# Gate rows by one transfer per expert, the second attention's outputs of every second group taken earlier, and the convolution's spectrum computed beside the gathers

## Chip, cores and metric

The kernel runs on one core of one Trainium2 chip, in single precision. The metric is the device time of one execution in microseconds (us), the median of several runs. Lower is better.

## What is computed

A two-layer decoder on x (4 sequences of 512 tokens, 256 features), with a layer norm after each residual sum:

```python
x = _layernorm(x + _L0_attn_ref(x, ...))      # attention among a token's 16 heads
x = _layernorm(x + _L0_xattn_ref(ctx, x, ...)) # cross attention to 64 context rows
x = _layernorm(x + _L0_ffn_ref(x, ...))       # 8 experts, two per token
x = _layernorm(x + _L1_attn_ref(x, ...))      # causal, 16 heads, top 64 scores kept, heads mixed before and after
x = _layernorm(x + _L1_xattn_ref(x, ctx, ...)) # modulation, S4D convolution, an MLP of 1024
x = _layernorm(x + _L1_ffn_ref(x, ...))       # 64 small experts, eight per token, plus 2 shared experts
```

Three places matter here. The last feed-forward part computes, for every token, all 64 experts of width 64 (silu(x W1 + b1) W2) and weighs each with the token's gate, which is zero for all but eight. The second attention mixes the 16 heads' scores with a 16x16 matrix, keeps the 64 largest of each row, and mixes the heads again after the softmax. The S4D part convolves the sequence with a kernel K of 512 positions by 256 features; that is done by a discrete Fourier transform as a matrix product, for which the spectrum of K (1024 rows: real and imaginary parts) is needed.

## The kernel before

The program is a row of stages, each a block in which all engines run their own instruction stream, with a barrier at the end. Semaphores order the engines within a block. SyncE (SP) issues nearly all DMAs, in the order of its program; a wait on it holds up everything behind it.

**Combining stage of the first feed-forward part** (`l0_combine`, line 2514). GpSimd issues 32 gathers of 128 rows of 1 KB (line 2528). TensorE meanwhile sums the convolution kernel K from small factors (512 matmuls with 16 columns, line 2538); VectorE copies each of 8 groups to `kl` (line 2547). Then VectorE weighs the gathered rows (lines 2553 and 2557). SyncE writes `kl` to DRAM (line 2563).

**Second attention** (`l1_attention`, from line 1502). Each batch has four tiles of 128 queries. A group is one tile; `ORDER = (0, 3, 1, 2)` gives the tiles at positions 0 to 3, so the narrowest tile (keys 24 to 144) comes first. A group has 8 steps (`STEPS1`), each with a pair of row blocks of 128 rows (8 queries by 16 heads). In step k TensorE mixes the scores of pair k+2 (`mix`), does side work (`l1_units`: projections, values and scores of tiles to come), transposes the pair k-2 with the second mixing (`post`, line 1745), and then takes finished groups' products: `heads` (attention weights times values, lines 1763 and 1767) and `output` (lines 1778 to 1780: eight products with the output weights, the bias, the residual). ScalarE does the matching copies in the same order; the copy of an output is line 1909, and `mixed_out` (line 1861) stands behind it in the next step. VectorE searches the 64 largest (lines 2049 to 2074), GpSimd masks (lines 2003, 2011). Two functions set when the products of a group come: `l1_heads(k)` and `l1_outs(k)` (lines 1483 and 1496). A group at position 0 has its heads in steps 2 to 5 and its output in step 6 of the next group; a group at another position has its heads in steps 1 to 7 of the next group and its output in step 0 of the one after that. The last group's products come at the end.

**Spectrum** (`s4d_spectrum`, line 2088). A stage of its own after the second attention's norm: SyncE loads `kl` back (512 KB) and the transform's matrix `dft` (2 MB), TensorE multiplies them in 8 groups of 4 products (line 2115; each shows as two matmul records), ScalarE copies each group to `kf` (line 2106). `modulation_attention` (line 2120) follows.

**Last stage** (`l1_tail`, line 2594). First the MLP of the modulated branch (hidden products line 2780, output line 2794), with the router between. ScalarE's first copy to `xT` (line 2883) waits for all twelve loads counted on `small_in`. Then a loop over 4 batches of 40 items: 8 of the shared experts and 32 pairs of small experts. Of one item TensorE computes the hidden values (line 2807: 128 hidden rows, two experts of 64, by 512 tokens), ScalarE applies the activation (line 2912), VectorE multiplies by the gates for a pair (line 3043), and TensorE adds the output product (line 2826) two items later. After the last item of a batch comes the bias product (line 2832). The gates stand in DRAM as one row of 512 values for each expert; for each pair SyncE copies two of them, each onto 64 partitions, into one of four buffers (line 2717). It may do so once the pair four earlier has been multiplied (semaphore `ready`). SyncE's same program stores the gates of batches 1 to 3 (line 2699) and writes the results of finished batches (line 2703).

Of the kernel before, what the change touches and what calls it, by code (L numbers as in the profile page):

```python
# [7 lines left out]
F32 = mybir.dt.float32  # L8
# [6 lines left out]
P = 128  # L15
B, S, D = 4, 512, 256
NT = S // P
# [1465 lines left out]
def l1_heads(k):  # L1483

    n = k // STEPS1 - 1
    s = k % STEPS1
    if n < 0 or n >= GROUPS1:
        return []
    if n == GROUPS1 - 1:
        return [(n, j) for j in range(8)] if s == 1 else []  # L1490
    if n % NT == 0:
        return [(n, 2 * (s - 2) + a) for a in range(2)] if 2 <= s < 6 else []
    return [] if s == 0 else [(n, s - 1)] if s < STEPS1 - 1 else [(n, s - 1), (n, s)]


def l1_outs(k):

    n, s = k // STEPS1 - 1, k % STEPS1
    if n >= 0 and n % NT == 0 and s == 6:
        return [n]  # L1500
    if n >= 1 and s == 0 and (n - 1) % NT != 0 and n - 1 < GROUPS1 - 1:
        return [n - 1]
    return []
# [584 lines left out]
def s4d_spectrum(nc, G, kf):  # L2088

    with ExitStack() as ctx:  # L2090
        sb, ps, sem = buffers(nc, ctx, "ss")
        kl = sb("kl", [P, NT, D])
        dft = sb("dft", [P, NT, 2 * FR])
        pf = [ps(f"pf{i}", [P, 512]) for i in range(2)]
        loaded, spectrum, stored = sem("loaded"), sem("spectrum"), sem("stored")
        with nc.Block() as block:
            @block.sync
            def _(sp):
                sp.dma_start(kl[:], G.s4d_positions.rearrange("p (j d) -> p j d", j=NT)).then_inc(loaded, 16)
                sp.dma_start(dft[:], G.dram["c_dft"].rearrange("(k p) f -> p k f", p=P)).then_inc(loaded, 16)  # L2100

            @block.scalar
            def _(act):
                for n in range(2 * FT):
                    act.wait_ge(spectrum, n + 1)
                    act.copy(kf[:, n, :], pf[n % 2][:, 0:D]).then_inc(stored, 1)

            @block.tensor
            def _(pe):
                pe.wait_ge(loaded, 32)  # L2110
                for m in range(2 * FT):
                    if m >= 2:
                        pe.wait_ge(stored, m - 1)
                    for k in range(NT):
                        ins = pe.matmul(pf[m % 2][:, 0:D], dft[:, k, m * P:(m + 1) * P], kl[:, k, :],
                                        start=(k == 0), stop=(k == NT - 1))
                    ins.then_inc(spectrum, 1)


def modulation_attention(nc, G, cT):  # L2120

    with ExitStack() as ctx:
# [26 lines left out]
        dve_steps, mixed, cstored = sem("dve_steps"), sem("mixed"), sem("cstored")  # L2149
# [13 lines left out]

# [336 lines left out]
def l1_modulated(nc, G):  # L2500
    d = G.dram
    with ExitStack() as ctx:
        kf = ctx.enter_context(nc.sbuf_tensor("l1_kf", [P, 2 * FT, D], F32))
        s4d_spectrum(nc, G, kf)
        cT = ctx.enter_context(nc.sbuf_tensor("l1_cT", [P, KD, B * S], F32))
        modulation_attention(nc, G, cT)
# [7 lines left out]
def l0_combine(nc, G, R, K):  # L2514

    with ExitStack() as ctx:
        sb, ps, sem = buffers(nc, ctx, "sp")
        kl = sb("kl", [P, NT, D])
        pk = [ps(f"pk{i}", [LO, 32, HI]) for i in range(2)]
        summed, copied, stored, weighed = sem("summed"), sem("copied"), sem("stored"), sem("weighed")  # L2520
        N = D // 32
        y = R.w1[:].rearrange("p e k f -> p (e k f)")[:, 0:TOP0 * TT * D].rearrange("p (n t d) -> p n t d", n=TOP0, t=TT)
        with nc.Block() as block:
# [67 lines left out]
def l1_tail(nc, G, store):  # L2591


    with ExitStack() as ctx:
# [33 lines left out]
        mlp_in, expert_in, w2_in, small_in = sem("mlp_in"), sem("expert_in"), [sem(f"w2_in{i}") for i in range(2)], sem("small_in")  # L2628
# [38 lines left out]
        with nc.Block() as block:  # L2667
            @block.sync
            def _(sp):
                sp.dma_start(wm1[:], d["L1_xattn_W1"].rearrange("(k p) n -> p k n", p=P)).then_inc(mlp_in, 16)  # L2670
                sp.dma_start(wm2[:], d["L1_xattn_W2"].rearrange("(k p) n -> p k n", p=P)).then_inc(mlp_in, 16)
                with nc.allow_non_contiguous_dma(reason="biases and gains onto partitions"):
                    for i, v in enumerate(("L1_xattn_g_ffn", "L1_xattn_b_ffn")):
                        sp.dma_start(gf[:, i, :], d[v].rearrange("(k p) -> p k", p=P)).then_inc(small_in, 16)
                    sp.dma_start(bm1[:], d["L1_xattn_b1"].rearrange("(k p) -> p k", p=P)).then_inc(small_in, 16)
# [30 lines left out]
                for r in range(B * PAIRS):  # L2706
# [19 lines left out]
            def _(pool):  # L2726
                pool.memset(cw[E1:, :], 1.0).then_inc(ones, 1)
                pool.wait_ge(ones, 1)
                pool.wait_ge(small_in, 16 * 12)
# [6 lines left out]
            def _(pe):  # L2736
# [108 lines left out]
                pe.wait_ge(small_in, 16 * 12)  # L2845
# [24 lines left out]
            def _(act):  # L2870
# [45 lines left out]
                act.wait_ge(small_in, 16 * 12)  # L2916
# [18 lines left out]
                turned("n2", 2)  # L2935
                for x in range(B * ITEMS):
# [15 lines left out]
            def _(dve):  # L2952
# [99 lines left out]
                dve.wait_ge(small_in, 16 * 12)  # L3052
# [29 lines left out]
def build(nc, dram, out):  # L3082
    with ExitStack() as ctx:
        G = Shared(nc, ctx, dram)
        G.s4d_positions = nc.dram_tensor("s4d_positions", (P, NT * D), F32).ap()
# [40 lines left out]
```

## Time and profile before

| | |
|---|---|
| median of 3 runs | 4064.18 us (4058.31 to 4065.22) |
| the profiled execution's own time | 4035.73 us |
| its span | 4033.9 us |
| mean granted TensorE clock | 0.811 of full speed |
| TensorE matmuls busy | 2853.6 us (71%) |
| VectorE busy | 2492.0 us (62%) |
| ScalarE busy | 1079.2 us (27%) |
| GpSimd busy | 975.2 us (24%) |
| DMA | 234.80 MB, mean 58 GB/s |

The stages that the change touches, by the timeline:

| stage | from, us | to, us |
|---|---|---|
| combining | 1025.8 | 1075.5 |
| second attention | 1097 | 2670 |
| spectrum | 2688.0 | 2714.7 |
| modulation's attention | 2714.7 | about 2881 |
| last stage, MLP | 3138.6 | 3291 |
| last stage, items of 4 batches | 3291 | 4025.2 |

Busy times are sums over stages with different limits, so they don't say what an edit is worth. The chain of waits, the timeline around a boundary and the table of stretches do. Full speed of TensorE's clock is 2.4 GHz; the other level is half of it.

### The profile page before, as it was taken

To read this page: it belongs to the slowest core of one execution; us is meant where nothing else is said; L and a number is where in the kernel's file an instruction comes from. 1 tells how busy PE (TensorE), PEld (TensorE's weight loads), DVE (VectorE), ACT (ScalarE), POOL (GpSimd) and SP (SyncE) were. 2 spreads that over 40 slices of the span, in tenths; PEclk is the share of its full clock that TensorE was granted. 3 is DMA by queue.
4 is the path that set the end of the run, shared out by engine and by line. 5 is a ranking of instruction groups with operands and counts; after the bars stand their busy time and mean duration, and the time that the engine had idled before them with its cause. 6 is when DMAs were issued, how large, how long until landed. Compare 5 with 4: busy or idle time off the path is not lost. (4 is left out here: it accounts for less than half of the span.)

```text
span 4033.9 us, 40612 instructions
## 1 busy us (share of the span) xinstructions
PE 2853.6 (71%) x11696; PEld 1813.1 (45%) x11696; DVE 2492.0 (62%) x7770; ACT 1079.2 (27%) x2754; POOL 975.2 (24%) x1217
## 2 busy tenths in 40 slices
PE   4755982999586777577767766453279798878686
PEld 2323552676443445355445544341124465545453
DVE  4995654454329998998999899938744251111111
ACT  1013550343033333333333433211100231111111
POOL 2650003000314544454445445410031100000000
PEclk6657995999667788786878786775589899999998
DMA  2000003555232111212212211000010311111111
GB/s 83 0 0 14 6 1 136 160 164 169 83 101 69 55 64 57 84 41 77 71 53 64 69 58 45 19 31 1 9 53 0 89 58 53 45 54 45 54 49 46
DMA packets 177338, 234.80 MB, mean 58 GB/s; under 512 B 32089, under 2 KB 135197, under 8 KB 177118
## 3 DMA queue, kind: packets, MB, share of 16 engines
q1 hardware_dynamic: 174046, 223.81, 17.0%
q0 software_dynamic: 3072, 8.39, 0.7%
q8 instruction: 97, 1.59, 0.2%
q14 instruction: 123, 1.01, 0.1%
HBM read 170.56 MB, written 61.60 MB: 58 GB/s over the span
## 5 line engine op out<-in xcount | busy, mean ns | idle before, releaser
L2062 DVE MATCH_REPLACE8 a_rest<-a_best,a_rest 128x416 f32<-128x416 f32 (+54 forms) x1308 | 606.1, 472 | 0.0
L2070 DVE MAX8 a_best<-a_rest 128x8 f32<-128x416 f32 (+54 forms) x1308 | 567.4, 476 | 0.0
L3043 DVE TENSOR_TENSOR tl_hT<-tl_act_out,tl_gate 128x512 f32<-128x512 f32 x128 | 88.6, 692 | 570.2 <-DMA tl_gate<-l_gates 450.6
L1745 PE MATMUL a_pat<-a_kp,a_probs 128*128 128x128 f32 x1344 | 281.7, 380 | 210.9 <-POOL a_kp L1964 205.6
L1745 PEld LDWEIGHTS a_pat<-a_kp,a_probs 128*128 128x128 f32 x1344 | 248.9, 277 | 292.1 <-POOL a_kp L1964 267.9
L2003 POOL TENSOR_SCALAR a_probs<-a_mixed,a_best 128x120 f32<-128x120 f32 (+12 forms) x208 | 285.9, 1375 | 329.3 <-DVE a_best L2074 308.5
L2826 PE MATMUL tl_py<-tl_w,tl_hT 128*128 128x256 f32 x1024 | 258.5, 397 | 139.0 <-DVE tl_hT L3043 139.0
L1726 PE MATMUL a_psc<-a_kT,branch 64*128 64x264 f32 (+3 forms) x640 | 226.0, 609 | 182.5 <-ACT a_stage L1828 181.8
L2826 PEld LDWEIGHTS tl_py<-tl_w,tl_hT 128*128 128x128 f32 x1024 | 192.2, 194 | 251.0 <-DVE tl_hT L3043 209.9
L1726 PEld LDWEIGHTS a_psc<-a_kT,branch 64*128 64x128 f32 x640 | 118.7, 261 | 273.1 <-ACT a_stage L1828 247.2
L2807 PE MATMUL tl_ph<-xT,tl_w 128*128 128x512 f32 x512 | 240.8, 593 | 0.0
L1736 PE MATMUL a_pmix<-a_rows,a_kpre 128*128 128x264 f32 (+41 forms) x528 | 183.1, 475 | 79.1 <-ACT a_mixed L1861 74.5
L1964 POOL TENSOR_SCALAR a_kp<-a_kpost,a_rden 128x128 f32<-128x128 f32 x256 | 152.6, 608 | 318.1 <-DVE a_rden L2033 318.0
L2912 ACT ACTIVATE tl_act_out<-tl_ph,tl_b 128x512 f32<-128x512 f32 x128 | 88.0, 687 | 493.3 <-PE tl_ph L2807 490.5
L1880 ACT ACTIVATE a_probs<-a_probs,a_negmax 128x72 f32<-128x72 f32 (+28 forms) x232 | 126.2, 545 | 332.5 <-POOL a_probs L2011 329.7
L2011 POOL TENSOR_TENSOR a_probs<-a_mixed,a_probs 128x72 f32<-128x72 f32 (+28 forms) x232 | 185.0, 818 | 9.3
L2049 DVE MAX8 a_best<-a_mixed 128x8 f32<-128x24 f32 (+28 forms) x232 | 95.4, 454 | 116.6 <-ACT a_negmax L1868 58.4
L1414 DVE COPY xT<-f_pT 128x512 f32<-128x512 f32 x78 | 50.3, 686 | 174.5 <-PE f_pT L1346 174.5
L1736 PEld LDWEIGHTS a_pmix<-a_rows,a_kpre 128*128 128x128 f32 x528 | 98.8, 222 | 118.9 <-issue 109.1
L1828 ACT COPY a_stage<-a_psc 128x264 f32<-128x264 f32 (+3 forms) x320 | 112.1, 381 | 127.0 <-PE a_psc L1726 121.7
L1336 PE MATMUL f_ph<-f0o_w,f_xsT 128*128 x312 | 142.8, 601 | 0.6 <-issue 0.6
L1356 PE MATMUL f_py<-f_w,xT 128*128 128x256 f32 x624 | 141.1, 379 | 0.5 <-DVE xT L1414 0.5
(421 smaller groups left out, 5309.5 us busy)
## 6 DMA issues: line engine op xcount, KB each, us to landing
f_w<-in_L_ffn_W SPq DMA_DIRECT2D x39, 1024.0 KB, 5.7
tl_gate<-l_gates SPq DMA_DIRECT2D x128, 256.0 KB
l_scores<-a_stage SPq DMA_DIRECT2D x32, 528.0 KB, 2.7
l_scores<-a_stage SPq DMA_DIRECT2D x32, 400.0 KB, 2.4
l_scores<-a_stage SPq DMA_DIRECT2D x32, 272.0 KB, 2.1
f0o_w<-in_L_ffn_W SPq DMA_DIRECT2D x8, 1024.0 KB, 12.5
sorted_x<-z_blank SPq DMA_DIRECT2D x1, 4992.0 KB, 17.0
f_xs<-sorted_x SPq DMA_DIRECT2D x39, 128.0 KB, 5.3
```

What stands on the lines that cost most here:

```text
L1336: ins = pe.matmul(ph[half][:], xsT[:, j % 2, k, :], w, start=(k == 0), stop=(k == KD - 1))
L1356: ins = pe.matmul(py[j % 2][:], hT[j % 2][:, f, :], w2[:, j % 2, f, :], start=(f == 0), stop=(f == FT - 1))
L1726: full(pe.matmul(out[:, 0:hi - lo], qT[r, j, i * P:(i + 1) * P], kT[r, j, lo:hi], start=True, stop=True))
L1736: ins = pe.matmul(pmix[:, at, 0:hi - lo], kpre[:], rows[:, g % 4, lo:hi], start=True, stop=True)
L1745: ins = pe.matmul(pat[:, at + c, :], probs[:, g % 4, c * P:(c + 1) * P], kp[:, g % 4, :], start=True, stop=True)
L1964: pool.tensor_scalar(kp[:, g % 4, :], kpost[:], rden[:, g % 4:g % 4 + 1], None, ALU.mult).then_inc(kp_ready, 1)
L2003: ins = pool.tensor_scalar(p, x, best[:, a, LAST, 7:8], HIDE, ALU.is_lt, ALU.mult)
L2011: pool.tensor_tensor(p, x, p, ALU.add).then_inc(masked, 1)
L2062: last[a] = signal(dve.match_replace(rest[:, a, 0:wd], best[:, a, q - 1, :], rows_of[a] if q == 1 else rest[:, a, 0:wd], GONE))
L2070: last[a] = signal(dve.max(best[:, a, q, :], rest[:, a, 0:wd]))
L2807: ins = pe.matmul(ph[m % 2][:], lhsT, G.xT[:, k, b * S:(b + 1) * S], start=(k == 0), stop=(k == KD - 1))
L2826: ins = pe.matmul(py[t][:, 0:D], src[:, t * P:(t + 1) * P], w, start=(n == 0), stop=False)
```

## The change

Five edits in one file:
1. The gates of a pair are copied by two transfers, one per expert, each from one row of 512 values onto 64 partitions; VectorE waits for 32 instead of 16 on the buffer's semaphore.
2. In `l1_heads` and `l1_outs` the test `n % NT == 0` becomes `n % 2 == 0`: groups at position 2 follow the scheme of position 0.
3. The spectrum's products and copies move into `l0_combine`; `kl` isn't written to DRAM any more, the spectrum (1 MB) is.
4. The spectrum's stage goes, and `modulation_attention` loads `kf` behind its own loads, with a wait at the end of SyncE's program.
5. In `l1_tail` the three small loads that ScalarE's first copy needs are issued first and counted on a semaphore of their own.

```diff
@@ l1_heads, l1_outs
-    if n % NT == 0:
+    if n % 2 == 0:
         return [(n, 2 * (s - 2) + a) for a in range(2)] if 2 <= s < 6 else []
...
-    if n >= 0 and n % NT == 0 and s == 6:
+    if n >= 0 and n % 2 == 0 and s == 6:
         return [n]
-    if n >= 1 and s == 0 and (n - 1) % NT != 0 and n - 1 < GROUPS1 - 1:
+    if n >= 1 and s == 0 and (n - 1) % 2 != 0 and n - 1 < GROUPS1 - 1:
         return [n - 1]
@@ s4d_spectrum
-def s4d_spectrum(nc, G, kf):
...
@@ modulation_attention, behind the masks' loads
+                sp.dma_start(kf[:].rearrange("p n d -> p (n d)"), G.s4d_spectrum).then_inc(kf_in, 16)
+                sp.wait_ge(kf_in, 16)
@@ l0_combine
+        room = R.w1[:].rearrange("p e k f -> p (e k f)")
+        Y, T = TOP0 * TT * D, NT * 2 * FR
+        y = room[:, 0:Y].rearrange("p (n t d) -> p n t d", n=TOP0, t=TT)
+        dft = room[:, Y:Y + T].rearrange("p (k f) -> p k f", k=NT)
+        kf = room[:, Y + T:Y + T + 2 * FT * D].rearrange("p (n d) -> p n d", d=D)
...
+                pe.wait_ge(dft_in, 16)
+                pe.wait_ge(copied, N)
+                for m in range(2 * FT):
+                    if m >= 2:
+                        pe.wait_ge(kept, m - 1)
+                    for k in range(NT):
+                        ins = pe.matmul(pf[m % 2][:, 0:D], dft[:, k, m * P:(m + 1) * P], kl[:, k, :],
+                                        start=(k == 0), stop=(k == NT - 1))
+                    ins.then_inc(spectrum, 1)
+            @block.scalar
+            def _(act):
+                for m in range(2 * FT):
+                    act.wait_ge(spectrum, m + 1)
+                    act.copy(kf[:, m, :], pf[m % 2][:, 0:D]).then_inc(kept, 1)
...
-                sp.wait_ge(copied, N)
-                sp.dma_start(G.s4d_positions, kl[:].rearrange("p j d -> p (j d)")).then_inc(stored, 16)
+                sp.dma_start(dft, G.dram["c_dft"].rearrange("(k p) f -> p k f", p=P)).then_inc(dft_in, 16)
+                sp.wait_ge(kept, 2 * FT)
+                sp.dma_start(G.s4d_spectrum, kf.rearrange("p n d -> p (n d)")).then_inc(stored, 16)
                 sp.wait_ge(stored, 16)
@@ l1_tail, SyncE
+                    for i, v in enumerate(("L1_xattn_g_ffn", "L1_xattn_b_ffn")):
+                        sp.dma_start(gf[:, i, :], d[v].rearrange("(k p) -> p k", p=P)).then_inc(gain_in, 16)
+                    sp.dma_start(bm1[:], d["L1_xattn_b1"].rearrange("(k p) -> p k", p=P)).then_inc(gain_in, 16)
                 sp.dma_start(wm1[:], d["L1_xattn_W1"].rearrange("(k p) n -> p k n", p=P)).then_inc(mlp_in, 16)
                 sp.dma_start(wm2[:], d["L1_xattn_W2"].rearrange("(k p) n -> p k n", p=P)).then_inc(mlp_in, 16)
-                        sp.dma_start(gf[:, i, :], d[v].rearrange("(k p) -> p k", p=P)).then_inc(small_in, 16)
-                    sp.dma_start(bm1[:], d["L1_xattn_b1"].rearrange("(k p) -> p k", p=P)).then_inc(small_in, 16)
...
-                    sp.dma_start(gate[:, r % 4, :],
-                                 G.l1_gates[b, 2 * n:2 * n + 2, :].unsqueeze(1).to_broadcast([2, F1, S])
-                                 ).then_inc(gate_in[r % 4], 16)
+                    for e in range(2):
+                        sp.dma_start(gate[F1 * e:F1 * e + F1, r % 4, :], G.l1_gates[b, 2 * n + e].partition_broadcast(F1)
+                                     ).then_inc(gate_in[r % 4], 16)
@@ l1_tail, ScalarE (and TensorE, GpSimd, VectorE: 16 * 12 becomes 16 * 9)
-                act.wait_ge(small_in, 16 * 12)
+                act.wait_ge(gain_in, 48)
                 turned("nf", 0)
...
                 turned("n2", 2)
+                act.wait_ge(small_in, 16 * 9)
                 for x in range(B * ITEMS):
@@ l1_tail, VectorE
-                    dve.wait_ge(gate_in[r % 4], 16 * (r // 4 + 1))
+                    dve.wait_ge(gate_in[r % 4], 32 * (r // 4 + 1))
```

## Rows read from the trace of the kernel before

**Rows 1.** The chain that ended last, last stage: start us, us, what.

```profile
3345.19 1.73 PE tl_py L2826 x8
...
3472.05 1.99 PE tl_py L2826 x8
...
3654.50 1.99 PE tl_py L2826 x8
...
3659.94 1.73 PE tl_py L2826 x8
3663.38 1.73 PE tl_py L2826 x8
...
3836.49 1.99 PE tl_py L2826 x8
...
4018.00 3.78 PE tl_py L2826 x8
4021.78 3.43 PE tl_py L2832 x8
```

**Rows 2.** Stretches, last stage: length, busy PE, PEld, DVE, ACT, POOL, clock, DMA share, GB/s.

```profile
3462.00:3472.00 10.00, 6.78 (x23) 3.80 (x21) 1.38 (x2) 1.38 (x2) 0.00 (x0) 1.00 0.13 49
...
3510.00:3654.00 144.00, 109.04 (x353) 66.15 (x352) 18.93 (x28) 20.62 (x30) 0.00 (x0) 0.99 0.14 53
```

**Rows 3.** ScalarE at a batch boundary (start us, us, instruction), then a line of waits.

```profile
1524.64 0.61 ACT L1880 ACTIVATE a_probs<-a_probs,a_negmax 128x376 f32<-128x376 f32 x1 [3.52 <-POOL a_probs L2011]
...
1539.91 0.62 ACT L1880 ACTIVATE a_probs<-a_probs,a_negmax 128x392 f32<-128x392 f32 x1 [2.60 <-POOL a_probs L2011]
...
1549.90 0.37 ACT L1909 COPY x<-a_pO 128x256 f32<-128x256 f32 x1 [4.63 <-PE a_pO L1780]
...
ACT x L1909 <- PE a_pO L1780: 72.8, 16, 5.3
```

**Rows 4.** Timeline of SyncE, first issue of the spectrum's stage and of the next.

```profile
2687.97 0.32 SPq L2099 DMA_DIRECT2D ss_kl<-s4d_positions  x1
...
2714.72 0.38 SPq L2155 DMA_DIRECT2D ma_wq<-in_L_xattn_Wq  x1
```

**Rows 5.** Timeline, first 20 us of the last stage.

```profile
3139.53 0.57 SPq L2674 DMA_DIRECT2D tl_gf<-in_L_xattn_g_ffn  x1
...
3141.93 3.43 SPq L2676 DMA_DIRECT2D tl_b<-in_L_ffn_b  x1
...
3147.63 0.21 ACT L2875 ACTIVATE tl_std<-tl_rstd 128x12 f32<-128x12 f32 x1 [6.73 <-DVE tl_rstd L2963]
...
3157.76 1.45 ACT L2883 ACTIVATE xT<-tl_pT,tl_gf 128x512 f32<-128x512 f32 x2 [9.91 <-DMA tl_b<-in_L_ffn_sb]
```

**Rows 6.** DMA issues: destination and source, queue, count, KB of each, us to landing.

```profile
tl_wm<-in_L_xattn_W SPq DMA_DIRECT2D x2, 1024.0 KB, 6.5
...
s4d_positions<-sp_kl SPq DMA_DIRECT2D x1, 512.0 KB, 2.8
...
xa_bo<-in_L_xattn_bo SPq DMA_DIRECT2D x1, 128.0 KB, 2.9
```

**Rows 7.** Line 2717 (shortest, median and longest issue in ns), then one issue in the timeline.

```profile
L2717 SPq DMA_DIRECT2D tl_gate<-l_gates x128: 482/5222/6296, 3296.6 to 3997.5; - x128
...
3318.47 0.48 SPq L2717 DMA_DIRECT2D tl_gate<-l_gates  x1
```

**Rows 8.** Stretches (columns as in rows 2), combining stage and the spectrum's products.

```profile
1040.00:1054.00 14.00, 12.68 (x238) 12.57 (x236) 4.81 (x18) 0.00 (x0) 10.41 (x12) 0.50 0.36 105
...
2697.00:2701.00 4.00, 4.00 (x10) 3.19 (x11) 0.00 (x0) 0.28 (x1) 0.00 (x0) 0.50 0.00 0
2701.00:2714.00 13.00, 12.76 (x56) 10.76 (x54) 0.00 (x0) 2.53 (x8) 0.00 (x0) 0.94 0.00 0
```

**Rows 9.** Timeline, end of the combining stage.

```profile
1053.91 0.32 SPq L2563 DMA_DIRECT2D s4d_positions<-sp_kl  x1
...
1069.10 6.42 DVE L2557 SCALAR_TENSOR_TENSOR branch<-f0o_w,f0o_gates,branch 128x256 f32<-128x256 f32 x16
```

More of the change, by code:

```diff
@@ L2085, with modulation_attention @@
 FT = FR // P
-def s4d_spectrum(nc, G, kf):
[L2090 to L2120, printed above, removed]
+def modulation_attention(nc, G, cT, kf):
     with ExitStack() as ctx:
@@ L2148, in modulation_attention @@
             sem("scored"), sem("shifted"), sem("exped"), sem("meaned"), sem("turned"), sem("stored"))
-        dve_steps, mixed, cstored = sem("dve_steps"), sem("mixed"), sem("cstored")
+        dve_steps, mixed, cstored, kf_in = sem("dve_steps"), sem("mixed"), sem("cstored"), sem("kf_in")
         d = G.dram
@@ L2503, in l1_modulated @@
         kf = ctx.enter_context(nc.sbuf_tensor("l1_kf", [P, 2 * FT, D], F32))
-        s4d_spectrum(nc, G, kf)
         cT = ctx.enter_context(nc.sbuf_tensor("l1_cT", [P, KD, B * S], F32))
-        modulation_attention(nc, G, cT)
+        modulation_attention(nc, G, cT, kf)
         norm_stage(nc, G, "ni", add=False, turn=False, dst=G.branch)
@@ L2519, in l0_combine @@
         pk = [ps(f"pk{i}", [LO, 32, HI]) for i in range(2)]
+        pf = [ps(f"pf{i}", [P, 512]) for i in range(2)]
         summed, copied, stored, weighed = sem("summed"), sem("copied"), sem("stored"), sem("weighed")
+        dft_in, spectrum, kept = sem("dft_in"), sem("spectrum"), sem("kept")
         N = D // 32
-        y = R.w1[:].rearrange("p e k f -> p (e k f)")[:, 0:TOP0 * TT * D].rearrange("p (n t d) -> p n t d", n=TOP0, t=TT)
+        room = R.w1[:].rearrange("p e k f -> p (e k f)")
[3 more added lines that the diff above has]
+        kf = room[:, Y + T:Y + T + 2 * FT * D].rearrange("p (n d) -> p n d", d=D)
         with nc.Block() as block:
@@ L2627, in l1_tail @@
         pT = [ps(f"pT{i}", [P, S]) for i in range(2)]
-        mlp_in, expert_in, w2_in, small_in = sem("mlp_in"), sem("expert_in"), [sem(f"w2_in{i}") for i in range(2)], sem("small_in")
+        mlp_in, expert_in, w2_in = sem("mlp_in"), sem("expert_in"), [sem(f"w2_in{i}") for i in range(2)]
+        gain_in, small_in = sem("gain_in"), sem("small_in")
         moments, rooted, h_ready, x_ready = sem("moments"), sem("rooted"), sem("h_ready"), sem("x_ready")
@@ L2669, in _ @@
             def _(sp):
+                with nc.allow_non_contiguous_dma(reason="biases and gains onto partitions"):
+                    for i, v in enumerate(("L1_xattn_g_ffn", "L1_xattn_b_ffn")):
+                        sp.dma_start(gf[:, i, :], d[v].rearrange("(k p) -> p k", p=P)).then_inc(gain_in, 16)
+                    sp.dma_start(bm1[:], d["L1_xattn_b1"].rearrange("(k p) -> p k", p=P)).then_inc(gain_in, 16)
                 sp.dma_start(wm1[:], d["L1_xattn_W1"].rearrange("(k p) n -> p k n", p=P)).then_inc(mlp_in, 16)
                 sp.dma_start(wm2[:], d["L1_xattn_W2"].rearrange("(k p) n -> p k n", p=P)).then_inc(mlp_in, 16)
-                with nc.allow_non_contiguous_dma(reason="biases and gains onto partitions"):
-                    for i, v in enumerate(("L1_xattn_g_ffn", "L1_xattn_b_ffn")):
-                        sp.dma_start(gf[:, i, :], d[v].rearrange("(k p) -> p k", p=P)).then_inc(small_in, 16)
-                    sp.dma_start(bm1[:], d["L1_xattn_b1"].rearrange("(k p) -> p k", p=P)).then_inc(small_in, 16)
+                with nc.allow_non_contiguous_dma(reason="biases onto partitions"):
                     sp.dma_start(b1[:], d["L1_ffn_b1"].rearrange("(n a) h -> (a h) n", a=2)).then_inc(small_in, 16)
@@ L2728, in _ @@
                 pool.wait_ge(ones, 1)
-                pool.wait_ge(small_in, 16 * 12)
+                pool.wait_ge(small_in, 16 * 9)
                 for b in range(B):
@@ L2844, in _ @@
                 turn("n2", 0)
-                pe.wait_ge(small_in, 16 * 12)
+                pe.wait_ge(small_in, 16 * 9)
                 scores(0)
@@ L3051, in _ @@
                     normal_h(b)
-                dve.wait_ge(small_in, 16 * 12)
+                dve.wait_ge(small_in, 16 * 9)
                 dve.wait_ge(biased, 1)
@@ L3084, in build @@
         G = Shared(nc, ctx, dram)
-        G.s4d_positions = nc.dram_tensor("s4d_positions", (P, NT * D), F32).ap()
+        G.s4d_spectrum = nc.dram_tensor("s4d_spectrum", (P, 2 * FT * D), F32).ap()
         G.sorted_x = nc.dram_tensor("sorted_x", (SLOTS * P, D), F32).ap()
```

## The prediction

> **What bounds the kernel now.** I read the chain that ended last, then the stretches it names. Its largest link is the transfer of the gates in the last stage, and the chain's rows give a ruler for it: the output product of one item (line 2826) starts every 3.44 us where only TensorE sets the pace (3659.94 to 3663.38) [rows 1]. The last products of the four batches start at 3472.05, 3654.50, 3836.49 and 4018.00: 182.45, 181.99 and 181.51 us for 40 items each, or 4.55 us an item. So TensorE waits there. The table of stretches says for what [rows 2]: between 3510 and 3654 it is busy 109 of 144 us at a granted clock of 0.99, while the DMA engines are busy 0.14 and move 53 GB/s. One gate transfer is 256 KB, so at that rate it takes 4.9 us, and 5.3 at the 49 that the shorter stretches show; VectorE's product waits for it. A share of 0.14 is about two of sixteen engines (0.125): the source's slowest dimension is 2 (two experts), its next 64. Two engines are full and fourteen idle.
>
> In the second attention the timeline shows a different bound: VectorE's search, except where one batch ends and the next begins with the narrowest tile. There TensorE computes the output of the third group, ScalarE waits for it, and the narrow tile's rows wait behind ScalarE [rows 3]. The spectrum's stage [rows 4] has nothing beside it. At the last stage's start ScalarE waits for twelve small loads of which it needs three [rows 5].
>
> **Gates.** 128 transfers of 2x64 rows become 256 of 64 rows of 2 KB. If the slowest dimension sets the number of engines, as the two busy ones say, 64 rows can lie on all sixteen, four on each. I cost the pace at TensorE's 3.44 us, if the pair of transfers lands in less. Bounds for the pair: a broadcast of 128 KB onto 128 partitions landed 2.9 us after its issue [rows 6]; two in flight at once take that, two strictly in turn 5.8. They are issued up to four items ahead (13.8 us), so latency is covered and only the rate counts; the pair of 1024 KB loads landed in 6.5 us [rows 6], or 1.6 for each 256 KB, latency and all. I take the pace as TensorE's, nearer 2.9, and keep the other end for a rival. SyncE: an issue that finds room takes 0.48 us, though the median of the 128 is 5.22 [rows 7]; I read the 5.22 as standing in a full queue, since the same instruction was short where it had waited for a buffer. Two are 0.96 of 3.44 us. The three stores of gate weights and the four stores of results stand in the same queue and get short with it; VectorE's wait for 32 instead of 16 queues nothing else.
>
> A batch then takes 39 x 3.44 plus the 5.44 us between 3654.50 and 3659.94, where the bias product lies: 139.6 us. Savings: 182.45 - 139.6 = 42.9, then 42.4 and 41.9. In the first batch I count 26 steps of one item from 3345.19 to 3472.05: 126.86 - 26 x 3.44 = 37.4, less 1 for the transposes of weights between them: 36.4. At the very end TensorE runs at the half clock, since it had waited: the last two groups took 3.78 and 3.43 us, the first of them 1.99 at the end of the other batches [rows 1]. Half of 7.2, 3.6, is gained. Sum **167.2**.
>
> Against it stands a rule. The Trainium skill, "DMA: Bandwidth & Descriptors", rules for kernel authors, says that two transfers to disjoint partition halves are not worth it, as both spray over the same engines and serialize. The same list says that a small slowest dimension confines a transfer to that many engines. The share of 0.14 [rows 2] speaks for the second; the first would leave this term at nothing, and it is a rival below.
>
> **Attention.** In groups at position 2 of four, the heads move from steps 1 to 7 to two each in steps 2 to 5 of the following group, and the output from the next group's step 0 to step 6. Nothing is added: 16 products with the weights, the bias and the residual, one ScalarE copy. Before, ScalarE sat idle 4.63 us for it at 1549.90 and then copied for 0.37; all sixteen outputs took 72.8 us of such waits, none over 5.3 [rows 3]. Four of them are moved from exposed places, three at boundaries and one in the drain, where the last posts queue behind it on TensorE: 4 x 5.0 = 20.0.
> The new place is covered by VectorE's search, whose steps are 15 us long there (1524.64 to 1539.91). At those two points ScalarE waits 3.52 and 2.60 us for GpSimd's mask [rows 3]; the output's 5.0 at the end of step 6 uses these up, but step 7 loses two heads and a copy. What could be late next is the narrow tile's first mixed rows. I give back 1 us over all: **19**. Bounds: 0 (the wait merely moves) and 21; a loss if TensorE there is at the half clock, 10 us for an output instead of 5, of which 4 could show at each of four places.
>
> **Spectrum.** Removed: the stage from SyncE's first issue at 2687.97 to the next stage's first at 2714.72 [rows 4], **26.75** us, nothing lying beside it. The next stage's first products wait for their own loads as before. Added there: a load of 1024 KB behind the masks' loads on SyncE, with a wait at the end of its program; its landing, 6.5 us by the load of that size [rows 6], lies in the stage that begins at 2714.72 and is 166 us long by the table of stages. Added in the combining stage: the load of 2 MB, the 32 products (two matmul records each), 8 copies and a store of 1 MB. The load has the 28 us from the stage's start to 1053.9; the gathers are paced by GpSimd's issue, and it can push the early ones only. The products start when VectorE's last copy is done (SyncE's issue at 1053.91 marks it) and there, as in the removed stage, they begin at the half clock, 0.50 [rows 8]. In the removed stage they took 4.00 + 12.76 us of TensorE, 0.50 in the first part and 0.94 in the second [rows 8]; with the last copy 17.2. So 1071.1, then issue and landing of the store: 2.8 us by the 512 KB stored here before, 6.5 by the load of 1024 [rows 6]; I take 4.6, halfway: 1076. VectorE is done at 1069.10 + 6.42 = 1075.5 [rows 9]. Cost **1**. If the clock stayed low, the work of 4.00 x 0.50 + 12.76 x 0.94 = 14 us at full clock would take 28, ending at 1087: 11. At best it is 0; a gain is excluded, since VectorE's part is untouched.
>
> **Small loads.** ScalarE's wait goes from 3157.76 to where the second root is done, 3147.63 + 0.21 [rows 5]: 9.9. The weights of the first layer are issued 2.4 us later (the moved issues filled 3139.53 to 3141.93), so the second leaves at 3141.4 and lands, by the same pair's 6.5 us [rows 6], at 3147.9; TensorE needs them when ScalarE's 1.45 us are over, at 3149.3. Descriptors of 4 bytes ahead of them may cost a microsecond. Gain **9**, between 5 and 9.9. The rest of the stage follows TensorE, so it shifts whole. GpSimd and VectorE still wait for the nine others, needed 30 us later.
>
> **Sum.** 167.2 + 19 + 26.75 - 1 + 9 = 221 of the profiled run's 4035.7 (span 4033.9 and 1.8 around it): 3814.7. The three runs have a median of 4064.2, 28.5 above the profiled one; I carry that over: 3843. Were the 28.5 all in slower gate transfers, 3815.
>
> **Rivals.**
> 1. *Gates half freed*: many engines read one 2 KB row of DRAM, and a pair takes 4.4 us. For: 2.9 us for 128 KB is more than bytes explain. Against: it contains the fixed latency. Against 5.3 now and 3.44 forecast that loses half of 167: 3927.
> 2. *Nothing gained at the gates*: the two halves go through the same engines one after the other, so the pair takes 5.3 us as before; only 54 of gain are left: 4010. Against: fourteen idle engines. It is the first rule's case.
> 3. *The output only moves its wait*: VectorE starved in step 7, or the boundary late. Gain 0 to -16 in the attention: 3862 to 3878. For: slack of 2.6 and 3.5 us only. Against: the step loses two heads.
> 4. *Slower*: the 5.22 us of an issue are SyncE's own work for a broadcast, not a full queue. Two are 10.4 us an item, 128 items 1336 us instead of some 722: 614 - 54 more, 4624. It decides from 3.0 us an issue, where two would take 5.6 us, today's pace (722 / 128), and the 0.4 of an item that the 54 give. For: the median. Against: the issues of 0.48.
> 5. *The spectrum does not fit*: half clock, 11 us, and the last gather delayed by 4: 3857.
>
> **How the numbers follow.** Forecast 0.76, rivals 1: 0.07, 2: 0.05, 3: 0.06, 4: 0.02, 5: 0.04. The range takes the forecast with its bounds and rivals 3 and 5: down to 3808 (the 28.5 and a few us of the bounds), up to 3878. Rivals 1, 2 and 4 with 0.14 are outside. A measurement tells 0.2%, 8 us. Only rival 4 is slower; 0.01 for mishaps that cancel. Faster 0.97.
>
> **What would show it.** In the profile after: gate issues of 0.5 us, outputs every 3.44 us throughout and 139.6 us between the last products of two batches; VectorE waiting for ScalarE's activations, not for gates; DMA share above 0.14 with twice the transfers; no output of TensorE in the narrow tile's step 0; combining stage ended 0 to 2 us later; the modulation's stage begun 0.3 us after the norm; the first hidden product 10 us earlier. Outputs at 5.34 would refute the reading of the engines, issues of 5 us that of the queue.

## The result, and the profile after

The changed kernel takes **3853.62 us** (median of 4 runs, 3849.98 to 3853.76), the kernel before 4064.70 beside it (4058.31 to 4069.04): a ratio of 0.948, 95% interval 0.9468 to 0.9492. The forecast was 3843, its range 3808 to 3878. The profiled execution took 3853.54 us.

| profile of | before | after |
|---|---|---|
| the execution's time | 4035.73 us | 3853.54 us |
| its span | 4033.9 us | 3851.7 us |
| mean granted TensorE clock | 0.811 | 0.800 |
| TensorE matmuls busy | 2853.6 us (71%) | 2838.4 us (74%) |
| VectorE busy | 2492.0 us | 2491.4 us |
| DMA | 234.80 MB, 58 GB/s | 235.88 MB, 61 GB/s |

Between these two profiles lie 182 us, between the medians 211. That difference is the main finding, and comes last here.

**Last stage.** The chain of waits of the kernel after, as [rows 1] (L2819 is the output product, L2825 the bias product):

```profile
3421.15 1.73 PE tl_py L2819 x8
3424.59 1.73 PE tl_py L2819 x8
3426.32 1.73 PE tl_py L2825 x8
3429.76 1.73 PE tl_py L2819 x8
...
3565.78 1.73 PE tl_py L2825 x8
...
3705.24 1.73 PE tl_py L2825 x8
...
3841.28 1.74 PE tl_py L2825 x8
```

Outputs come every 3.44 us, batches every 139.46, 139.46 and 136.04 us. The stretch of the second batch (columns as in [rows 2]), then the gates' issues (as [rows 7]) with their time to landing, then the waits of VectorE's product:

```profile
3430.00:3564.00 134.00, 134.00 (x468) 88.66 (x468) 25.19 (x45) 29.40 (x42) 0.00 (x0) 1.00 0.20 67
```
```profile
L2711 SPq DMA_DIRECT2D tl_gate<-l_gates x256: 444/592/1489, 3285.0 to 3824.3; - x128
...
DMA to landing us min/median/max: 2.7/2.9/4.0
```
```profile
DVE tl_hT L3037 <- ACT tl_act_out L2905: 385.8, 126, 14.1
```

TensorE is busy all of the 134 us. An issue lasts 0.59 us instead of 5.22, with twice as many of them, and a gate row lands in 2.9 us. VectorE waits for ScalarE's activations alone.

**Attention.** ScalarE at the same boundary as [rows 3]:

```profile
1564.43 0.37 ACT L1909 COPY x<-a_pO 128x256 f32<-128x256 f32 x1 [5.54 <-PE a_pO L1780]
...
1578.01 0.62 ACT L1880 ACTIVATE a_probs<-a_probs,a_negmax 128x392 f32<-128x392 f32 x1 [2.57 <-POOL a_probs L2011]
...
1583.28 0.34 ACT L1861 ACTIVATE a_mixed<-a_pmix 128x56 f32<-128x56 f32 x2
```

The narrow tile's row of 56 keys in the kernel before:

```profile
1550.17 0.34 ACT L1861 ACTIVATE a_mixed<-a_pmix 128x56 f32<-128x56 f32 x2
```

The output is now copied at 1564.43, ahead of step 7. From the activation of 392 keys to the narrow tile's mixed row of 56 keys it takes 5.27 us; before, the output stood between them and it took 10.26 (1539.91 [rows 3] to 1550.17).

**Combining stage.** The stretches of line 2513, the 512 small products (length, busy PE, PEld, clock, DMA share, GB/s), and the stage's end:

```profile
1026.00:1036.00 10.00, 4.50 (x59) 3.62 (x57) 0.50 0.81 303
1036.00:1066.00 30.00, 3.43 (x22) 2.29 (x22) 0.50 0.36 105
1066.00:1076.00 10.00, 6.87 (x121) 6.66 (x122) 0.50 0.01 2
1076.00:1090.00 14.00, 14.00 (x266) 14.00 (x265) 0.50 0.01 2
```
```profile
1091.58 16.57 PE L2522 MATMUL sp_pf<-sp_kl,f0o_w 128*128 128x256 f32 x64 [1.35 <-DVE sp_kl L2537]
...
1095.67 6.41 DVE L2547 SCALAR_TENSOR_TENSOR branch<-f0o_w,f0o_gates,branch 128x256 f32<-128x256 f32 x16
...
1108.59 0.32 SPq L2554 DMA_DIRECT2D s4d_spectrum<-f0o_w  x1
...
1113.35 1.23 DVE L143 TENSOR_TENSOR x<-x,branch 128x1024 f32<-128x1024 f32 x1 [11.27 <-PEq L82]
```

Only 22 products run in the 30 us from 1036, and the last 266 run in 14 us. The products take 66.0 us (1024.0 to 1090.0); in the profile of before they took 26.7 (1025.8 to 1052.5). The spectrum's products follow, and the next stage's addition begins at 1113.35, where it had begun at 1076.31.

**Modulation's stage and the MLP's start.** The first issues, the load of the spectrum and the first products; then the last stage's start, as [rows 5]:

```profile
2710.95 0.38 SPq L2123 DMA_DIRECT2D ma_wq<-in_L_xattn_Wq  x1
...
2712.73 2.43 SPq L2129 DMA_DIRECT2D ma_tmask<-in_mask_BxS_bf  x4
2715.20 0.57 SPq L2131 DMA_DIRECT2D l_kf<-s4d_spectrum  x1
...
2721.57 4.88 PE L2142 MATMUL ma_pp<-xT,ma_wq 128*128 128x512 f32 x7 [11.50 <-DMA ma_tmask<-in_mask_BxS_bf]
```
```profile
3137.11 0.38 SPq L2664 DMA_DIRECT2D tl_gf<-in_L_xattn_g_ffn  x1
...
3146.16 0.21 ACT L2868 ACTIVATE tl_std<-tl_rstd 128x12 f32<-128x12 f32 x1 [6.74 <-DVE tl_rstd L2957]
3146.28 1.43 ACT L2876 ACTIVATE xT<-tl_pT,tl_gf 128x512 f32<-128x512 f32 x2
...
3147.86 2.90 PE L2773 MATMUL tl_ph<-xT,tl_wm 128*128 128x512 f32 x3 [4.78 <-ACT xT L2876]
```

In the kernel before, the last stage's first issue was not the one that [rows 5] begin with but that of the MLP's weights, 0.94 us earlier:

```profile
3138.59 0.38 SPq L2670 DMA_DIRECT2D tl_wm<-in_L_xattn_W  x1
```

The MLP's first product comes 10.75 us behind the stage's first issue; it was 20.76 (3159.35, 3138.59). The first products of the modulation's attention come 10.6 us behind theirs; in the trace of before they began at 2722.03, 7.3 us behind [rows 4].

### The profile page after: what moved, and what is told of

Its sections match the earlier page's. It is cut to its first block and busy times, and to the rows that moved or that the text cites. A ratio compares the mean times of both kernels' runs of the same rounds, so it can differ in the third digit from the quotient of the medians.

```text
span 3851.7 us, 40732 instructions
## 1 busy us (share of the span) xinstructions
PE 2838.4 (74%) x11696; PEld 1831.2 (48%) x11696; DVE 2491.4 (65%) x7770; ACT 1078.0 (28%) x2754; POOL 976.2 (25%) x1217
## 2 busy tenths in 40 slices
DMA packets 181179, 235.88 MB, mean 61 GB/s; under 512 B 35929, under 2 KB 139037, under 8 KB 180702
## 5 line engine op out<-in xcount | busy, mean ns | idle before, releaser
L1745 PE MATMUL a_pat<-a_kp,a_probs 128*128 128x128 f32 x1344 | 295.7, 395 | 206.1 <-POOL a_kp L1964 201.1
L1745 PEld LDWEIGHTS a_pat<-a_kp,a_probs 128*128 128x128 f32 x1344 | 262.4, 291 | 287.5 <-POOL a_kp L1964 263.4
L2819 PE MATMUL tl_py<-tl_w,tl_hT 128*128 128x256 f32 x1024 | 241.6, 379 | 0.0
L2819 PEld LDWEIGHTS tl_py<-tl_w,tl_hT 128*128 128x128 f32 x1024 | 194.6, 190 | 80.2 <-issue 60.0
## 6 DMA issues: line engine op xcount, KB each, us to landing
f_w<-in_L_ffn_W SPq DMA_DIRECT2D x39, 1024.0 KB, 5.6
f0o_w<-in_L_ffn_W SPq DMA_DIRECT2D x8, 1024.0 KB, 12.6
```

Source lines behind the costliest of these rows:

```text
L1745: ins = pe.matmul(pat[:, at + c, :], probs[:, g % 4, c * P:(c + 1) * P], kp[:, g % 4, :], start=True, stop=True)
L2819: ins = pe.matmul(py[t][:, 0:D], src[:, t * P:(t + 1) * P], w, start=(n == 0), stop=False)
```

## The experiments

They ran in three series, each with its own runs of the kernel before. The median of those was 4062.61 us (7 runs) beside experiments 1 to 4, 4035.13 (13 runs) beside 5 to 8, and 4034.48 (6 runs) beside 9 to 12. The changed kernel takes 3853.62 us beside the first of these medians and 3812.72 beside the last (experiment 9). The expectations of 5 to 8 add to 3853.6, but these four ran in the second series, so their differences are taken here from 3812.72. Stage lengths come from the timelines; "combining" is from the first small product to the addition of the next stage.

**1. The kernel before again** (no edit).

> The kernel before, unchanged, to see its combining stage a second time. In the profile of before TensorE's 512 small products took 27 us and the stage 50.5 us to the norm's first addition; in the changed kernel the same products took 65 us, idle up to 2.6 us before each with nothing shown that they wait for, until the last gather had landed, and the stage took 89. Theory A (the gathers hold up TensorE's stream of instructions, and the profile of before was the exception): the small products take 60 to 66 us here too, the stage 77 to 80, and the time is near 4064, not 4036. Theory B (the new load of 2 MB causes the hold-up): products 27 us, stage 50.5, time near 4036 or a difference elsewhere.

4064.21 us, a single run. The same line (L2538 here) in its trace:

```profile
1036.00:1066.00 30.00, 3.27 (x21) 2.12 (x19) 0.50 0.34 101
1066.00:1076.00 10.00, 7.80 (x139) 7.49 (x139) 0.50 0.01 2
```

Where the profile of before has 313 products in those 30 us, this one of the same kernel has 21. Its combining stage takes 78.9 us instead of 50.5. The 28.4 us are the size of the 28.5 that the forecast had carried over without a cause (the other stages differ by up to 5.6 us and sum to 0.3), and they aren't the change's doing. Small products that stand idle like this are called the hold-up below.

**2. Spectrum undone**: the stage of its own, the store of `kl` and its reload are back, the rest stays changed.

```diff
+        s4d_spectrum(nc, G, kf)
-                sp.dma_start(kf[:].rearrange("p n d -> p (n d)"), G.s4d_spectrum).then_inc(kf_in, 16)
```

> The changed kernel with the spectrum back in its own stage; gates, attention and small loads stay changed. Theory A: the small products are held up as in the changed kernel; the stage loses only the spectrum behind them, 89 to some 78 us, and the spectrum's stage costs 26.75 again: 3853.6 + 26.8 - 11 = 3869. Theory B: the stage is back at 50.5 us: 3853.6 + 26.8 - 38.8 = 3841.6.

3862.76 us, ratio 0.951 (0.9494 to 0.9526). Combining takes 78.9 us; from the attention's last output to the modulation's first issue 44.8 us pass instead of 17.5, and from there to the MLP 433.5 instead of 436.9. So here the moved spectrum costs 89.35 - 78.9 = 10.4 us, gains 27.3, and the load of `kf` costs 3.4. Theory A holds; its 3869 is 6 too high for that load and for an attention of 1556.1 us against 1559.4.

**3. The transform's matrix loaded late**: the 2 MB only when the last small product is done.

```diff
+                sp.wait_ge(summed, N)
                 sp.dma_start(dft, G.dram["c_dft"].rearrange("(k p) f -> p k f", p=P)).then_inc(dft_in, 16)
```

> The changed kernel, with the load of the transform's matrix issued only when TensorE's small products are done. Theory A: they are held up by the gathers all the same until some 45 us after the stage's start; then the load (9 us) comes on top of the path: 3853.6 to 3862. Theory B: products in 27 us, load 9, spectrum 17, store 5: a stage of about 60 instead of 89, 3825.

3856.81 us, 0.9497 (0.9481 to 0.9513). The small products still take 66.1 us, with 22 of them in the 30 us from 1036: the 2 MB load doesn't hold TensorE up. Loaded late it only delays the spectrum, and combining takes 96.2 us. That is theory A.

**4. The gathers issued late**: after the last small product.

```diff
+                pool.wait_ge(summed, N)
                         pool.indirect_dma_start(y[:, n, t, :], None, G.sorted_y,
```

> The changed kernel, with GpSimd's gathers begun only when TensorE's small products are done; the load of 2 MB stays at the start. Theory A: products in 27 us although the load runs beside them; the gathers then take 27 to 69 us, the spectrum's products are held up by them in turn, and the stage ends after 76 to 91 us: 3840 to 3856. Theory B: the products are held up for the 10 us of the load and no longer: 37 us, then gathers to 79, stage 87 or more: 3851 or more.

**3841.00 us**, 0.9459 (0.9444 to 0.9475). Line 2514 here, with no gather beside it and the 2 MB load running:

```profile
1024.00:1036.00 12.00, 12.00 (x229) 12.00 (x228) 0.50 0.45 175
1036.00:1066.00 30.00, 13.53 (x254) 13.42 (x252) 0.69 0.19 54
```

All 512 are done in 26.5 us (1022.8 to 1049.3) and combining takes 77.15 us, though the gathers begin only then. So the gathers are what holds TensorE up, and where they do, this order beats both kernels: 12.6 us below the 3853.62 of the changed one.

TensorE isn't the only engine that stands still. Three of ScalarE's eight copies of the spectrum, which now run beside the gathers (in brackets the idle time before each; "remote" is the profile's word where it finds no engine or transfer of the kernel that released it):

```profile
1065.29 0.37 ACT L2531 COPY f0o_w<-sp_pf 128x256 f32<-128x256 f32 x1 [5.06 <-remote]
1074.44 0.37 ACT L2531 COPY f0o_w<-sp_pf 128x256 f32<-128x256 f32 x1 [8.78 <-remote]
1093.34 0.37 ACT L2531 COPY f0o_w<-sp_pf 128x256 f32<-128x256 f32 x1 [18.52 <-remote]
```

In experiment 11, with the same order and no hold-up, these copies come every 1.73 us. Here TensorE runs the first six groups of the spectrum in 12.4 us beside the gathers, and then it is TensorE that waits for ScalarE, 7.15 us before the last group. The copy at 1093.34 is of the seventh group, whose products had ended at 1067.71; the last gather is issued at 1088.62. The stage is hardly longer for it, 77.15 us here and 77.1 there: the store of the spectrum, issued at 1095.22, now ends it, at nearly the time when VectorE, which waits for the gathers until 1091.35, is done (1098.8).

**5. Gates undone**: one transfer of 2x64 rows for a pair again, and a wait for 16.

```diff
-                    for e in range(2):
-                        sp.dma_start(gate[F1 * e:F1 * e + F1, r % 4, :], G.l1_gates[b, 2 * n + e].partition_broadcast(F1)
+                    sp.dma_start(gate[:, r % 4, :],
+                                 G.l1_gates[b, 2 * n:2 * n + 2, :].unsqueeze(1).to_broadcast([2, F1, S])
```

> The changed kernel with one transfer of two rows per pair again, all else as changed. Theory (two engines of sixteen carry it): the 167 us come back, 3853.6 + 167 = 4021, with VectorE waiting for gates and a DMA share of 0.14 in the items. Rival (part of the gain belongs to the shorter queue for stores and results, or to the clock): less than 150 comes back.

3982.19 us, 0.9869 (0.9852 to 0.9885). The gates' issues and VectorE's wait, as before the change:

```profile
L2710 SPq DMA_DIRECT2D tl_gate<-l_gates x128: 482/5222/6372, 3244.1 to 3946.0; - x128
```
```profile
DVE tl_hT L3037 <- DMA tl_gate<-l_gates: 450.9, 97, 5.9
```

From the MLP's start to the last bias product 864.5 us, against 695.7 in experiment 7 beside it: the gates are worth 168.8 (169.5 in the medians). Less than 150 was the rival, and it falls.

**6. Attention undone**: the two functions with `% NT` again.

```diff
-    if n % 2 == 0:
+    if n % NT == 0:
```

> The changed kernel with position 2's heads and outputs where they were. Theory (four exposed outputs of 5 us): 3853.6 + 19 = 3872.6; the interval may tell 16 from 22. Rival (the output only moved its wait): 3854 to 3858. The second attention took 1578 us in the kernel before run again and 1555 to 1559 in four runs with the change, so I lean to 19 or a little more.

3834.44 us, 0.9503 (0.9487 to 0.9519). From the attention's first load of weights to its last output 1575.3 us, against 1557.0 to 1557.4 in experiments 5, 7, 8 and 9: 18 us (21.7 in the medians).

**7. ScalarE waits for all small loads again.**

```diff
+                act.wait_ge(small_in, 16 * 9)
```

> The changed kernel, where ScalarE waits for all twelve small loads again before its first copy in the last stage; their order stays changed. Theory: the wait alone is worth the 9 to 10 us: 3863. Rival (the order of the loads did it, or the weights of the MLP come later anyway): 3854 to 3857.

3826.17 us, 0.9485 (0.9469 to 0.9501). From the modulation's first issue to the MLP 448.3 us, against 436.6 to 436.8 in experiments 5, 6 and 8: in this order of loads the wait is worth 11.6 (13.5 in the medians). That is more than the change gained here, because the new order makes it longer: the first hidden product comes 22.51 us behind the stage's first issue, against 20.76 in the kernel before and 10.74 without the wait.

**8. Two transfers of 2x32 rows** for a pair, each from one row as in the change, but with a slowest dimension of 2.

```diff
-                        ... G.l1_gates[b, 2 * n + e].partition_broadcast(F1)
+                        ... G.l1_gates[b, 2 * n + e].unsqueeze(0).unsqueeze(0).to_broadcast([2, F1 // 2, S])
```

> The changed kernel with two transfers for a pair as changed, but each source written as 2 x 32 repetitions of the row instead of 64, so that its slowest dimension is 2. Theory (the slowest dimension sets the number of engines): back to two engines, the pace of an item 5.3 us or more, about 4021 us, DMA share 0.14. Rival (having two transfers in flight is what helps): as changed, 3854, DMA share the same as in the changed kernel. If the two repeated dimensions are folded into one of 64 before they reach the queue, this run tells nothing and shows 3854 too.

4005.57 us, 0.9939 (0.9922 to 0.9955). Issues, wait and a stretch (columns as in [rows 2]):

```profile
L2711 SPq DMA_DIRECT2D tl_gate<-l_gates x256: 482/2551/3787, 3243.5 to 3975.0; - x128
```
```profile
DVE tl_hT L3037 <- DMA tl_gate<-l_gates: 477.4, 99, 6.2
```
```profile
3462.00:3580.00 118.00, 95.97 (x315) 59.03 (x313) 15.91 (x23) 18.35 (x27) 0.00 (x0) 0.99 0.14 50
```

As many transfers as in the change, as many bytes, and a DMA share of 0.14 again: it isn't the number of transfers that frees the gates but their shape. This one is 24.5 us slower in the stage than the single transfer (889.0 against 864.5).

**9. The changed kernel again** (no edit).

> The changed kernel once more, on the chip of the next three kernels. Theory: there are two kinds of chip or run. Where the kernel before has its median near 4035, the 512 small products beside the gathers take 27 us, the combining stage 50.6 us and this kernel about 3816 (ratio 0.9455); where it has its median near 4063, they take 65 us, the stage 89 us and this kernel 3853 (ratio 0.948). Rival: the 28.5 us lie elsewhere, then the stage's length does not go with the median of the kernel before.

**3812.72 us**, 0.9448 (0.9431 to 0.9465), beside 4034.48 of before. Line 2513, then the stage's end:

```profile
1036.00:1066.00 30.00, 15.10 (x284) 14.99 (x282) 0.67 0.36 106
```
```profile
1052.44 15.83 PE L2522 MATMUL sp_pf<-sp_kl,f0o_w 128*128 128x256 f32 x64 [1.35 <-DVE sp_kl L2537]
...
1067.70 6.42 DVE L2547 SCALAR_TENSOR_TENSOR branch<-f0o_w,f0o_gates,branch 128x256 f32<-128x256 f32 x16
...
1068.71 0.32 SPq L2554 DMA_DIRECT2D s4d_spectrum<-f0o_w  x1
```

The hold-up isn't there: 26.6 us for the small products, 50.6 for the stage, where VectorE's part is again the last.

**10. The load of `kf` behind the masks.**

```diff
+                sp.wait_ge(loaded, 128)
                 sp.dma_start(kf[:].rearrange("p n d -> p (n d)"), G.s4d_spectrum).then_inc(kf_in, 16)
```

> The load of the spectrum (1 MB) in the modulation's stage is issued only when the eight loads in front of it have landed. Theory: that load pushes the landing of the masks; then the stage's first products start 7.3 us behind its first issue instead of 8.9 to 10.6, and the median is 2 to 3 us below the changed kernel's on this chip. Rival: the first products wait for the weights themselves or the queue's issue, and the time stays within 0.5 us.

3815.68 us, 0.9457 (0.944 to 0.9474), no faster than experiment 9. The first products come 7.3 us behind the first issue (2678.30, 2685.59) instead of 8.3, as the theory had it, and from the first issue to the MLP it takes 433.2 us instead of 436.3: the stages behind the edit are 3.1 us shorter. The median is 3 us above that of experiment 9 all the same, so that part of the expectation missed. In the profiles the stages ahead of the edit, which it doesn't touch, are 7.35 us longer (the modulation's first issue at 2678.30 instead of 2670.95), and why is not shown. The theory is borne out on the cause and on the stage, not on the time.

**11. Gathers late and `kf` behind the masks** (experiments 4 and 10 together).

> As the run before, and the gathers issued only when the last small product's group is copied. Theory: on a chip with the hold-up (kernel before near 4063) the combining stage takes 77 us instead of 89 and the median is 3838, 15 below the changed kernel; on a chip without it the stage takes 77 instead of 50.6 and the median is 24 us above the changed kernel, 3840. Rival: the order of gathers and products is worth the same on every chip.

3836.80 us, 0.951 (0.9493 to 0.9527). Combining takes 77.1 us instead of 50.6, and the kernel is 24.1 us slower than the changed one. The rival falls: with experiment 4, the order that gains where the hold-up is loses where it isn't. The first products of the modulation's stage come after 7.8 us, and the MLP after 435.7.

**12. Plain loads for the gathers**: the same sizes from the same queue, 128 rows in fixed order. It leaves out the choice of each token's own rows.

```diff
-                        pool.indirect_dma_start(y[:, n, t, :], None, G.sorted_y, ...
+                        pool.dma_start(y[:, n, t, :], G.sorted_y[x:x + P]).then_inc(G.fetched[t // NT], 16)
```

> The 32 gathers are replaced by 32 plain loads of the same sizes from GpSimd's queue, of 128 rows in a fixed order; left out is the choice of each token's own rows. Theory: it is the gathers' row-by-row descriptors that hold up TensorE; then the 512 small products take 27 us here on any chip, and on a chip with the hold-up the combining stage takes some 50 us less whatever the gathers took, the median some 28 to 38 us below the changed kernel. Rival: any transfer issued by GpSimd holds TensorE up, and the products take 65 us on such a chip as before. On a chip without the hold-up this run tells only how fast the plain loads land.

3812.72 us, 0.9447 (0.943 to 0.9464), combining 50.7 us. This series had no hold-up, so the run says nothing on which property of the gathers causes it. The issues came closer together (32 in 17 us instead of 39), and the stage still didn't get shorter: VectorE is done at 1065.4, and now the spectrum ends the stage, with its store issued at 1072.03 and the addition at 1076.80.

## Why the prediction was right, point by point

The forecast's 221 us stood on a profile without the hold-up, where it is best tested: 4034.48 to 3812.72 is **221.8**. By stages, first the profile of before against that of experiment 9, then, both with the hold-up, that of experiment 1 against the profile after:

| term | predicted | measured without the hold-up | with it |
|---|---|---|---|
| gates, MLP's start to last bias product | 167.2 | 865.3 - 694.7 = 170.6 | 862.2 - 694.7 = 167.5 |
| attention, first load to last output | 19 | 1572.7 - 1557.4 = 15.3; 18 by experiment 6 | 1578.3 - 1559.4 = 18.9 |
| spectrum, last output to modulation's first issue | 26.75 | 44.6 - 17.5 = 27.1 | 45.8 - 17.5 = 28.3 |
| spectrum's cost in the combining stage | -1 | 50.5 - 50.6 = -0.1 | 78.9 - 89.35 = -10.4 |
| modulation's first issue to the MLP | 9 | 444.6 - 436.3 = 8.3 | 444.2 - 436.9 = 7.3 |

Without the hold-up the two remaining stretches add 1.4, and the sum is 222.6 us to the last bias product; with it they take 0.9, and the sum is 210.7, against 211.1 between the medians. That 221.8 meets 221 to the microsecond is partly luck: the gates' term is 3.4 too low and the attention's 3.7 too high.

**Gates.** Right step by step: pace 3.44, issues 0.59 (called 0.5), a pair inside it. The term was 3.4 short, because the last batch's 139.6 took over a pace that holds only where the next batch's hidden products stand between the last outputs; it took 136.04. The kernel before itself varies by 3.1 in this stretch (865.3 and 862.2), so the 3.4 is no more than that. Rivals 1 and 2 fall with VectorE's wait, which is for ScalarE alone, and rival 4 with the issues of 0.59 us. The weighing of two rules of one page can now be settled. Experiment 8 has two transfers to disjoint partitions and stays at a DMA share of 0.14; the change has two such transfers, a share of 0.20 and no wait. The Trainium skill, "DMA: Bandwidth & Descriptors", "Why a DMA increments its semaphore by 16 and not by 1", says that the number of engines is the largest up to 16 that divides the slowest dimensions of both sides; the runs agree, with 2 for 2x64 and 2x32. The Trainium skill's rule on the same page, rules for kernel authors, that two transfers to disjoint partition halves aren't worth it did not hold here: it gives as its reason that both halves spray over all 16 engines either way, and here the one transfer that they replace lay on about two (a share of 0.14).

**Attention.** At one boundary the move gained 4.99 us (10.26 to 5.27), as costed. Over the stage profiles differ by more than the 4 us between 19 and 15.3: the kernel before took 1572.7 in one and 1578.3 in another. Rival 3, an output that only moves its wait, is refuted; the outputs' waits are as long as before (73.1 us for sixteen, 72.8 then [rows 3]) but lie beside VectorE's search.

**Small loads.** The first hidden product came 10.0 us nearer to the last stage's first issue (20.76 to 10.75), a little more than the term's 9 and its bound of 9.9; the list of signs had 10. The microsecond kept back for descriptors of 4 bytes was not lost. **A miss** is the sentence "The next stage's first products wait for their own loads as before": the load of the spectrum stands behind the masks' tiny loads on the queue, and the first products came after 8.3 to 10.6 us instead of 7.3, in every run that had it there. Experiment 10 ties it to that load. From the modulation's first issue to the last stage's it takes 425.4 to 427.4 us in all these runs, and 422.5 to 424.9 where the load isn't there or is held back (the profile of before and experiments 1, 2, 10 and 11). So the load cost 1.5 and 2.7 us in the two pairs of the table, and 3.1 and 3.4 by experiments 10 and 2. The prediction put this cost at nothing.

**Spectrum, and the offset.** The step that failed is a pair: carrying 28.5 us over without a cause, and reading the combining stage's 50.5 us as the stage's length in the timed runs. The timed runs beside the forecast were at the level of the hold-up, and there the stage takes 78.9 us before (experiment 1) and 89.35 after. The reason is a different bound. Without the hold-up VectorE's wait for gathers ends the stage and the spectrum's 16 us fit before it; with it the gathers are long done when the last small product is, VectorE needs only 10.6 us more (1091.5 to 1102.1), and the spectrum takes 17 us plus the store's landing (1091.58 to some 1112). So the change costs **10.4** there, not 1. Put it in the place of the 1 in 3843 and the forecast is 3852.4; measured were 3853.62. Rival 5 had that size, 11, for another reason, a clock that stays low, and is not borne out: the time was lost behind the small products, not in the spectrum's. No rival had the hold-up: that 3853.62 lies in the range is owed to the room made for an attention that gains nothing and for rivals 3 and 5, and that the 28.5 could be carried over whole, to both kernels having it alike. That much is luck.

**What stays open** is why a gather holds TensorE's stream up, and ScalarE's copies in experiment 4, and why in some series and not in others. Both kernels show it, in the runs beside the forecast and in the first series alike, at 4063 us; none does in the last two series, at 4035. The record names the chip of each experiment: 1 to 4 ran on one, 5 to 12 on another. So the hold-up may go with the chip; two chips don't show it, and for the profile of before, without the hold-up, and the timed runs beside it no chip is on record. The gathers themselves run alike in both, 32 issues in 39 us. In the hold-up the waits before single small products are put down to nothing that the profile shows. In the 30 us from 1036 the trace has two 16 KB packets of instructions where the products run free and none where they are held up, but a TensorE that runs fewer instructions also fetches fewer, so this doesn't say which causes which. A run of experiment 12 in a series with the hold-up would tell whether it is the indirection or GpSimd's queue; there is none.

## What to carry to other kernels

Read the number of engines off a transfer before its bytes: a share of 0.14 with everything waiting meant two engines of sixteen, and reshaping the slowest dimension, not splitting as such, gave 169 us of 4035. When the profiled execution and the median differ by more than the runs scatter, find the stage where they differ before adding a term: an offset of 28.5 us hid another bound in the very stage the change filled. Work put beside gathers is free only as long as the gathers end last; an order that gained 12.6 us in one series lost 24 in another, so one series doesn't settle it.

## What the runs showed of the hardware

- Gathers issued by GpSimd can hold up TensorE's stream of small products for as long as they last: in the changed kernel 22 products in 30 us beside them and 266 in 14 us behind them, but 284 in the same 30 us in experiment 9. The kernel before has 21 in one trace and 313 in another. A 2 MB load from SyncE's queue, moving 303 GB/s with the first gathers, isn't the cause (experiments 3 and 4).
- In the one trace where ScalarE has copies to make beside such gathers with the hold-up, it stands still too, up to 18.5 us before a copy of 0.37 us (experiment 4).
- 256 transfers of 64x2 KB from one row each keep up a pace of two per 3.44 us at a DMA share of 0.20; the same bytes as 2x32 rows don't, at 0.14.
- A load of 1 MB issued right behind four loads of 0.5 KB delays the products that wait for those: they start 8.3 to 10.6 us behind the stage's first issue, and 7.3 to 7.8 where the load is absent or held back.
